# A convolution and mixture-of-experts chain on one core: the second expert product made token-major, with its outputs taken back through HBM

## The reference

```python
x = x + _L0_conv_ref(_gn(x), ...)      # 3x3 convolution, 8 to 8 channels, bias
x = x + _L1_conv_ref(_gn(x), ...)      # the same, other weights
h = jnp.einsum('bend,edf->benf', x, w1) + b1    # _L2: expert = channel, token = row
out = jnp.einsum('benf,efd->bend', gelu(h), w2) + b2   # d = 256 columns, f = 1024
x = x + _L3_conv_ref(_gn(x), ...)      # a third 3x3 convolution
```

## Time and profile before

| | us |
|---|---|
| median of 3 runs (lowest, highest) | 577.23 (575.82, 577.95) |
| the profiled execution's own time | 576.91 |
| its span, first to last instruction | 575.1 |
| PE / DVE / ACT / POOL busy | 520.0 / 374.1 / 291.8 / 159.1 |
| mean granted TensorE clock | 0.971 |

### The profile page before, as it was taken

The page is one execution under the profiler, slowest core; times in us unless marked ns, Lnnn a source line. Parts: engine busy times, 40 slices in busy tenths (PEclk is TensorE's granted clock), DMA queues, the critical chain, the costliest instruction groups (busy, mean ns, idle before and its releaser), DMA issues.

```text
span 575.1 us, 9042 instructions
## 1 busy us (share of the span) xinstructions
PE 520.0 (90%) x3326; PEld 255.5 (44%) x3326; DVE 374.1 (65%) x644; ACT 291.8 (51%) x354; POOL 159.1 (28%) x181
## 2 busy tenths in 40 slices
PE   0879999896979999999999999999999989978990
PEld 0534445364544444444444444444444545445440
DVE  4969999888766395194293392481547598678541
ACT  2599988333635453353362361461444828766510
POOL 4679888853270000000000000000000001677610
PEclk9889999898899999999999999999999999989996
DMA  8845555533020122022011112102123300134769
GB/s 327 324 111 146 150 132 139 143 101 147 0 75 1 73 74 74 0 73 73 0 73 73 31 42 73 73 0 73 74 74 108 112 0 2 45 81 107 242 200 349
DMA packets 14168, 57.41 MB, mean 100 GB/s; under 512 B 3116, under 2 KB 3244, under 8 KB 11052
## 3 DMA queue, kind: packets, MB, share of 16 engines
q1 hardware_dynamic: 11820, 49.30, 26.9%
q10 hardware_dynamic: 2316, 7.68, 3.7%
HBM read 30.03 MB, written 8.39 MB: 67 GB/s over the span
## 4 chain that ended last, share of the span: by engine, by line
PE 62%; DVE 19%; ACT 5%; POOL 4%; DMA 3%; issue 2%; ACTq 1%; SPq 1%; POOLq 0%; DVEq 0%
PE PS L1007 28%; PE PS L978 27%; DVE X L665 6%; DVE ST L626 6%; PE PS L878 2%; POOL XN L360 2%; ACT XN L439 2%; PE PS L952 2%; DMA X<-x 2%; PE PS L936 2%; PE PS L885 1%; DVE X L681 1%; ACT SCR L444 1%; DVE XT L674 1%; DVE SM L641 1%
## 5 line engine op out<-in xcount | busy, mean ns | idle before, releaser
L978 PE MATMUL PS<-XT,W1S 128*128 (+1 forms) x768 | 172.0, 383 | 1.7 <-DVE XT L674 1.7
L1007 PE MATMUL PS<-HID,W2S 128*128 128x512 f16 x768 | 170.8, 379 | 1.6 <-DVE W2S L688 1.6
L476 ACT ACTIVATE SCR<-PS,CONST 128x512 f32<-128x512 f32 x128 | 87.0, 686 | 64.4 <-PE PS L978 27.8
L978 PEld LDWEIGHTS PS<-XT,W1S 128*128 128x128 f16 x768 | 75.6, 99 | 91.1 <-issue 4.7
L1007 PEld LDWEIGHTS PS<-HID,W2S 128*128 128x128 f16 x768 | 75.1, 98 | 87.5 <-issue 1.8
L360 POOL TENSOR_TENSOR XN<-SCR,XN 128x1024 f16<-128x1024 f32 (+1 forms) x61 | 100.4, 1670 | 26.5 <-ACT SCR L444 26.5
L688 DVE SCALAR_TENSOR_TENSOR W2S<-W2F,W2S 128x2048 f16<-128x2048 f32 x10 | 22.9, 2291 | 114.6 <-ACT W2S L472 114.6
L333 POOL MEMSET HALO<- 48x520 f16 x12 | 6.3, 526 | 316.8 <-PE PS L978 316.3
L626 DVE BATCH_NORM_STATS2 ST<-X 128x6 f32<-128x512 f32 x128 | 81.5, 681 | 9.4 <-DMA X<-x 8.2
L439 ACT ACTIVATE XN<-X,SC 128x1024 f16<-128x1024 f32 (+1 forms) x61 | 64.1, 1050 | 33.9 <-POOL SC L351 27.6
L665 DVE SCALAR_TENSOR_TENSOR X<-PS,X 128x512 f32<-128x512 f32 x96 | 59.7, 680 | 21.5 <-PE PS L900 21.5
(11 more groups left out here) (47 smaller groups left out, 442.9 us busy)
## 6 DMA issues: line engine op xcount, KB each, us to landing
W1F<-w SPq DMA_DIRECT2D x10, 1024.0 KB, 4.7
W2F<-w SPq DMA_DIRECT2D x10, 1024.0 KB, 4.8
HALO<-XN SPq DMA_DIRECT2D x48, 129.9 KB
out<-X ACTq DMA_DIRECT2D x12, 512.0 KB, 6.8
HALO<-XN SPq DMA_DIRECT2D x48, 121.8 KB
X<-x SPq DMA_DIRECT2D x2, 2048.0 KB, 19.0
HALO<-XN SPq DMA_DIRECT2D x42, 64.9 KB
HALO<-XN SPq DMA_DIRECT2D x42, 60.9 KB
```

The source lines that it names most:

```text
L476: act.activation(SCR[:, ft % 2, 0:CH], bank(ft % G_RING), ACT.Gelu, bias=BT[:, ds(e * FT + ft, 1)], scale=1.0 / (XS * WS)).then_inc(gelu_o ...
L978: mm = pe.matmul(bank(ft % G_RING), W1S[:, w, h * NF + ft * P:h * NF + (ft + 1) * P], rhs, start=(n == 0), stop=(n == 3 * DH - 1))
L1007: mm = pe.matmul(bank(G2_BANK + h), W2S[:, w, ft * NW + h * P:ft * NW + (h + 1) * P], HID[slot][:, part, ft], start=(ft == 0 and part == 0 ...
```

## The change

**Second product.** `output` now takes HID's 128 tokens as the stationary operand and w2's 256 columns as the moving one: for each expert and pair four blocks (4 rows x 32 row groups of one image) of 24 matmuls with 256 columns, 1536 in all for 768 with 512. ScalarE copies each block out of PSUM (`copy_out`), 64 copies of 128x256 for 32 of 128x512. The bias is no longer in it: VectorE adds it to X, eight adds of a chunk for each image, in four of the loop's rounds (`add_bias`). XT's layout puts an expert's 256 tokens side by side; the writes into it, and the reads of PSUM for them, step differently.

**The way back.** SP stores each block to a new HBM tensor `yd` (64 DMAs of 128 KB, runs of 512 bytes). Whole rows come back: seven experts' rows of an image by two DMAs in ScalarE's queue, the last expert's by two in SP's, into a float32 image over the dead part of XT. `add_outputs` adds from there, all operands in SBUF. The result transposes are gone.

**The end.** The third convolution has seven PSUM banks in its ring for five. The first half's thirds of g = 8 to 11 are issued by ScalarE, all else of the halos by SP. All output stores are in SP's queue: image 0 and half of image 1 between the halos of g = 10 and 11, the rest after them.

```diff
-TT = 2 * NT
+NBLK = 2
+TOK = NBLK * P
+BLOCKS = 2 * NBLK
...
-L3_BANKS = (1, 2, 3, 0, 4)
+G2_BANK, TR_BANK, STAT_BANK, LAST_STAT_BANK = 4, 6, 5, 6
+L3_BANKS = (1, 2, 3, 0, 7, 4, 5)
...
-THIRDS_BY_ACT = ((0, 0), (11, 0), (11, 1),)
+THIRDS_BY_ACT = ((0, 0), (8, 0), (9, 0), (10, 0), (11, 0))
...
-    XT = at("XT", XY_OFF, [P, NPAIR, TT, DH, NC, 2, R], F16)
-    YT = at("YT", XY_OFF, [P, NPAIR, TT, DH, NC, R], F32)
+    XT = at("XT", XY_OFF, [P, NB, DH, NE, 2, TOK], F16)
+    YT = at("YT", XY_OFF, [P, NB, NBLK, NE, NW], F32)
+    YX = at("YX", XY_OFF, [P, NB * IMG], F32)
...
+        b, t = m // NCH, m % NCH * TC
+        return XT[:, b, :, :, part].rearrange("p w c (r t) -> p (w c) r t", r=R)[:, :, :, t:t + TC]
     def tr_bank(m):
-        return bank(TR_BANK + m % 2).rearrange("p (k r) -> p k r", r=R)
-
-    def yt_part(e, p, dh):
+        return bank(TR_BANK + m % 2).rearrange("p (t k r) -> p k r t", t=TC, r=R)
...
+    def y_image(b):
+        return YX[:, (0, 1, 0, 3)[b] * IMG:((0, 1, 0, 3)[b] + 1) * IMG]
...
+    def load_outputs(queue, b, rows):
+        queue.dma_start(y_image(b)[rows], yd[b][rows]).then_inc(y_in[b], 16)
+    def load_first_experts(queue, b):
+        for w in range(W2):
+            load_outputs(queue, b, slice(w * HALF_P, (w + 1) * HALF_P - R))
+    def load_last_expert(queue, b):
+        for w in range(W2):
+            load_outputs(queue, b, slice((w + 1) * HALF_P - R, (w + 1) * HALF_P))
...
+        def store_tokens(src, b, k, e, signal):
+            rows = yd[b].rearrange("(w c k r) (t j) -> c k (r t) w j", w=W2, c=NC, k=NBLK, j=NJ)
+            dst = rows[e, k]
+            sp.dma_start(dst, src.rearrange("p (w j) -> p w j", w=W2)).then_inc(signal, 16)
+        def store_outputs(e, p, first):
+            for k in range(BLOCKS):
+                sp.wait_ge(yt_ok, first + k + 1)
+                store_tokens(y_tokens(e, p, k), 2 * p + k // NBLK, k % NBLK, e, y_out[p])
+        def store(b, first):
+            for i in range(first, first + QUAD, 2):
+                sp.wait_ge(x_new, X_NEW_AT["c", 8 + b, i + 1])
+                sp.dma_start(out[b][:, i * CH:(i + 2) * CH], x_chunk(b, i, 2)
+                             ).then_inc(out_done, 16)
+        def store_last(n, k):
+            p = ENDING[n][1]
+            b = 2 * p + k // NBLK
+            sp.wait_ge(yt_ok, BLOCKS * (NPAIR * LAST + n) + k + 1)
+            store_tokens(y_last(p, k), b, k % NBLK, NE - 1, last_out[b])
...
-        for e in range(1, NE + 2):
+        for e in range(1, LAST + 1):
             load_w1(e)
             load_w2(e)
-        for g in range(8, 12):
-            if g < 8 + SLOTS:
-                load_ones(SLOT[g])
-            halos(g)
+            for p in range(NPAIR):
+                store_outputs(e - 1, p, BLOCKS * (NPAIR * (e - 1) + p))
+        load_w1(LAST + 1)
+        load_w2(LAST + 1)
+        store_outputs(LAST, 0, BLOCKS * NPAIR * LAST)
+        load_w1(LAST + 2)
+        load_w2(LAST + 2)
+        for k in range(BLOCKS):
+            store_last(1, k)
+        for b in range(2):
+            sp.wait_ge(last_out[b], 16 * NBLK)
+            load_last_expert(sp, b)
+        load_w1(LAST + 3)
+        load_w2(LAST + 3)
+        store_outputs(LAST, 1, BLOCKS * (NPAIR * LAST + 2))
+        load_ones(0)
+        store_last(3, 0)
+        store_last(3, 1)
+        sp.wait_ge(last_out[2], 16 * NBLK)
+        load_last_expert(sp, 2)
+        halo_half(8, 0)
+        store_last(3, 2)
+        store_last(3, 3)
+        halo_half(8, 1)
+        sp.wait_ge(last_out[3], 16 * NBLK)
+        load_last_expert(sp, 3)
+        load_ones(SLOT[9])
+        halos(9)
+        load_ones(SLOT[10])
+        halos(10)
+        store(0, 0)
+        store(0, QUAD)
+        store(1, 0)
+        halos(11)
+        store(1, QUAD)
+        store(2, 0)
+        store(2, QUAD)
...
+        def copy_out(to, k, done):
+            act.wait_ge(g2_mm, done)
+            act.activation(to, bank(G2_BANK + k % 2)[:, 0:NW], ACT.Copy,
+                           scale=1.0 / (HS * WS)).then_inc(yt_ok, 1)
...
+        def first_experts(b, p):
+            if b != 2:
+                act.wait_ge(g1_mm, 16 * LAST + FT * (2 * p + 2))
+            act.wait_ge(y_out[p], 16 * BLOCKS * (NE - 1))
+            load_first_experts(act, b)
...
+                if (k, ft) == (3, 3):
+                    act.wait_ge(x_new, X_NEW_AT["y", 0, NCH - 1])
+                    first_experts(2, 1)
+            if k == 1:
+                first_experts(0, 0)
+                first_experts(1, 0)
+            elif k == 3:
+                first_experts(3, 1)
...
         slot_free(8)
         normalise_piece(FIRST_PIECE[8])
+        ending_out(3, 0)
         normalise_piece(FIRST_PIECE[8] + 1)
-        ending_result(3, 0)
+        ending_out(3, 1)
         normalise_piece(FIRST_PIECE[8] + 2)
         normalise_piece(FIRST_PIECE[8] + 3)
-        ending_result(3, 1)
+        ending_out(3, 2)
+        thirds(8, 0)
         normalise_piece(FIRST_PIECE[8] + 4)
-
...
-        for g in range(9, 11):
-            normalise(g)
-        store(0)
-        slot_free(11)
-        for k in range(4):
-            normalise_piece(FIRST_PIECE[11] + k)
-        last_thirds(0)
-        normalise_piece(FIRST_PIECE[11] + 4)
-        last_thirds(1)
-        for b in range(1, NB - 1):
-            store(b)
+        ending_out(3, 3)
+        for g in range(9, 12):
+            slot_free(g)
+            for k in range(4):
+                normalise_piece(FIRST_PIECE[g] + k)
+            thirds(g, 0)
+            normalise_piece(FIRST_PIECE[g] + 4)
...
+        def add_outputs(b, i):
+            if i == 0:
+                dve.wait_ge(y_in[b], 16 * 2 * W2)
             xc = x_chunk(b, i)
-            dve.wait_ge(ty_mm, m + 1)
-            dve.tensor_tensor(xc, bank(TR_BANK + m % 2), xc, ALU.add).then_inc(x_new, 1)
+            dve.tensor_tensor(xc, y_chunk(b, i), xc, ALU.add).then_inc(x_new, 1)
+        def mlp_stats(b, i):
             dve.wait_ge(x_new, X_NEW_AT["y", b, i])
-            stats_chunk(12 + b, xc, i)
+            stats_chunk(12 + b, x_chunk(b, i), i)
+        def add_half(b, first):
+            for i in range(first, first + QUAD):
+                add_outputs(b, i)
+            for i in range(first, first + QUAD):
+                mlp_stats(b, i)
+        def add_bias(e):
+            for i in range(NCH):
+                xc = X[:, ds(e * IMG - (IMG - i * CH), CH)].rearrange("p (t j) -> p t j", j=NJ)
+                dve.tensor_tensor(xc, xc, B2.unsqueeze(1).broadcast_to([P, TC, NJ]), ALU.add
+                                  ).then_inc(bias_ok, 1)
...
+            tokens = slice(k * P, (k + 1) * P)
+            to = bank(G2_BANK + k % 2)
             for ft in range(FT):
...
-                for part, w in ((0, 0), (1, 0), (0, 1)):
-                    mm = pe.matmul(bank(G2_BANK + h),
-                                   W2S[:, w, ft * NW + h * P:ft * NW + (h + 1) * P],
-                                   HID[slot][:, part, ft],
-                                   start=(ft == 0 and part == 0 and w == 0),
+                for part, w in PRODUCTS:
+                    mm = pe.matmul(to[:, 0:NW], HID[slot][:, part, ft, tokens],
+                                   W2S[:, w, ft * NW:(ft + 1) * NW],
+                                   start=(ft == 0 and part == w),
                                    stop=(ft == FT - 1 and w == 1))
+                if ft == FT - 1:
+                    mm.then_inc(g2_mm, 1)
                 if between is not None:
-                    if ft == FT - 1:
-                        mm.then_inc(g2_mm, 1)
-                    between(ft)
...
+        for n, (e, p, _) in enumerate(ENDING):
+            hidden(e, p, in_fourth_hidden if n == 3 else None, n)
+            for k in range(BLOCKS):
+                output(e, p, k, in_fourth_output if n == 3 else None, n)
+        for g in range(8, 12):
             before_step(g)
             for i in range(0, NCH, QUAD):
-                last_centres(g, i, None)
+                for k in range(QUAD):
+                    if g < 10 and i + k == NCH - 1:
+                        group_mean(g + 6)
+                    centre(g, i + k)
+                    if (g, i, k) == (8, 0, 0):
+                        group_variance(13)
+                if g < 10 and i > 0:
+                    group_variance(g + 6)
                 tiles(g, i)
```

More of the change, by code:

```diff
@@ L1022, in expert @@
             for p in range(NPAIR):
-                for h in range(DH):
-                    output(e, p, h)
+                for k in range(BLOCKS):
+                    output(e, p, k)
         pe.wait_ge(cst_in, 16)
```

373 lines of the change are left out of this document (160 added, 213 removed).

## The result

Four runs of the changed kernel gave 606.12 us (605.93 to 606.66), four of the kernel before 576.85 us (575.82 to 577.95). The ratio is 1.051, with a 95% interval of 1.049 to 1.053: slower, as forecast, but by 29 us where 5.5 were worked out, and outside the range of 572 to 591.

The account below looks back on a forecast made before the run. TensorE was taken to bound the loop, a ScalarE-GpSimd ring the third convolution and stores the end. Span 580.6 + 1.8 = 582.4 against 576.91, +5.5; 582.7 in the median's terms, range 572 to 591.

Parts of the forecast that it names:

- Step 1: Second product's stream: 1536 matmuls of 256 columns at 110 ns with weight loads hidden, +2.4 us up to the ending.
- Step 2: Loop's copies (0.5 us each), bias adds and 64 stores all hidden; XT's writes taken to cost nothing more.
- Step 3: Four ending parts up to the last hidden product: 77.5 us with stalls, ending at 485.9, a gain of 0.9 us.
- Step 4: Third convolution's ScalarE-GpSimd ring: four halo issues add 2.7 us per image for three images; last low part ends at 558.9.
- rival (a): Third convolution's ring is not lengthened, the halo issues being hidden: 8 us less there, time 573.3, faster; chance 0.20.
- Step 5: Last halo and stores: halos land 3 us later, updates end at 571.6, stores run until 576.9, span 580.6.
- (b): Third convolution's ring: half of the lengthening hidden, 578.0 us, no change; chance 0.17.
- Rival (c): Weight loads show in the output stream (598 at 120 ns) or XT's writes double (593); together 0.07.
- Rival (d): VectorE's SBUF adds and GpSimd's low parts lock each other out, 5.4 us into the ring: 588; chance 0.06.
- Rival (e): Image 2's last rows return late, some 6 us trip; each us beyond 503 costs one; within forecast's range, no separate chance.

Follow-up runs that it names:

- e1: Changed kernel without the round trip: no stores or loads of rows, VectorE adds the chunk to itself; 585.38 us.
- e8: e1 with the third convolution's halo issues and output stores back in the queues used before the change; 580.29 us.
- e4: Changed kernel with the third convolution's halo issues and output stores back in the queues used before the change; 599.53 us.
- e11: VectorE alternates adds and statistics for images 2 and 3, against a combined kernel with image 2's load split (583.00 us); 580.60 us.
- e15: e14 with image 3's last stores ahead of the first image's halo issues and its load between their halves; 579.60 us, ratio 1.0049.
- e12: e11 with ScalarE taking the last ending part's first two output copies before the first normalisation piece, the other two earlier; 580.35 us, ratio 1.0074.
- e13: e12 with image 2's bulk load asked for earlier, over before the last expert's stores; 579.58 us, ratio 1.0047.
- e6: Changed kernel without 56-partition bulk loads: each image returns in one 128-partition load after its last stores land; 592.84 us.
- e14: e12 with image 2 loaded whole behind its stores and no bulk load; 579.57 us.
- e9: Adds as scalar_tensor_tensor instead of tensor_tensor, against a kernel combining the orders of e2, e3, e4 and e6's whole loads (585.97 us); 582.39 us.
- e2: Changed kernel with the last ending part's weight loads ahead of SyncE's waits for the landed stores; 602.71 us.
- e3: Changed kernel with image 1's variance ahead of the first adds of image 2 on VectorE; 602.74 us.
- e5: Changed kernel with VectorE's first adds of image 0 after the third ending part's splits and the next weight split; 608.31 us.

## Why the prediction was wrong

The direction, the loop and the ring were right; the trip was not.

- *Step 1, the output stream.* 109.2 ns a matmul for the 110 taken, 20.96 us a stage. Weight loads (99 ns) stayed hidden. The formula of the Trainium skill, "TensorE: Matmul & The Clock Gate", section "Back-to-back issue gap", gives 109.2 for 256 columns, though the section means it for a single matmul alone. The rows of this stream agree with it.
- *Step 2.* XT's writes still took 684 ns, the 256-wide copies 384 ns, where I had taken 500, and the bias adds had no idle time before them. Its clause on the stores, that SP has nothing else waiting but weight loads, needed a stage later, is true of the loop only.
- *Step 3, the four parts.* Without the trip the stalls were sized well: e1 begins the last output at 484.4, where the forecast, less 1.9 us for the loads' issues that e1 does not make, has 484.0. That its first piece then came at 489.1, near the 490.1 forecast, is in part luck. It waited 2.97 us for GpSimd's scale, which the forecast did not have (2.01 before), and e1 does not make the issues for which the forecast had 3.1 us. With the trip the piece came at 501.9. I had gone through part 3 for what is late next and found the splits, but not that the change puts two new waits there: VectorE's for the rows, ahead of the last splits, and SyncE's for the landed stores, ahead of the weights. With what followed from these two the first piece came 11.8 us later than forecast, and 14.6 later than in e1 if both are counted from the split (314.4 and 299.8).
- *Step 4, the ring.* The four issues between the fourth and fifth piece cost what was forecast (2.7 to 2.8 us). e1's distances sum to 56.1 us for the 53.5 forecast, and its last low part ends 17.8 us after the last first piece instead of 15.3, as the halo issues there took 5.31 us for 2.7. SyncE issues six output stores just before (from 549.1 us) and its own halo copies beside them, and the stores I had not counted: with the end as before (e8) it is 15.3 us again (541.18 to 556.50). That these stores are the reason is likely and not shown, as e8 moves the issues too. Undone, the two moves together give back 6.4 us (e8) or 7.6 (e4), where the three images of rival (a) had 8.
- *Step 5.* From the end of the last low part to the end of the span: 20.5 us in e1 and 20.5 in the changed kernel, for 21.7. It was 1.2 us too long. Rivals (a) and (b) are refuted with step 4.
- *Rival (c)* is refuted by the rows of steps 1 and 2. *Rival (d)*, adds and low parts locked, is real and had too small a chance: VectorE's adds of images 2 and 3 do fall beside low parts. In e8 it is where the loss against the kernel before lies, and e11 took 3.2 us of it away by order alone. In the last versions it is the likeliest reason of what is left (e15's rows); no run is free of it. The row that it rested on, is a step of a group's scale on 128x1, not a subtraction.
- *Rival (e), the step that failed.* It had one of the two right places and a wrong size. I took "some 6 us" for store, landing and load; in the changed kernel it was 9.22 + 0.33 + 6.55 us, from a copy that came late itself, and the rows of image 2 arrived at 523.3. For images 0 and 1 the sum had nothing, and there the trip cost the 11.8 us of step 3. In all it is worth 22.1 us (e1). The rate, "each us beyond 503 is a us", is not borne out in the one pair that bears on it (its end as before): between e12 and e13 the rows came 7.7 us sooner, 2.0 of them beyond 503, and the stretch is 0.2 shorter. I counted the bytes of the DMA in the loop and never asked what the bulk loads do to the small stores sharing the DMA engines with them. Rival (e) deserved a chance and a price of its own.
- *In sum.* The span is 603.8 us for the 580.6 forecast, 23.2 too long: 19.0 by the trip (22.1 for the 3.1 forecast), 5.8 by the other steps (e1 against the forecast, both from the split), less 1.6 as the split came earlier (187.5 for 189.1).

The cause of that size is shown by e6, e12, e13 and e14. A load of 56 partitions moved 193 to 195 GB/s with a busy share of 0.87 to 0.88; loads of 128 partitions (rows and weights) 410 to 429 at 0.97 to 1.01. While such a load lasts, a small store in another queue is late: 8.0 us for 1.9. How the engines share their time between the two queues, no run shows. The Trainium skill, "SBUF — State Buffer", section "Door 1: The DMA port swizzle", says that partitions 0 to 63 reach only 8 of the 16 ports that DMA has into SBUF, and gives 196 GB/s for such a transfer of 1 MiB; its part on issuing two transfers for the two halves says that they do not add up. Both agree with the rows. The Trainium skill, "DMA: Bandwidth & Descriptors", section "Why a DMA increments its semaphore by 16 and not by 1", has a transfer run on the largest number of engines up to 16 that divides its partitions; for 56 that is 14 of 16, a share of 0.875 (an estimate by that rule). The rows have that share. The prediction weighed neither, and the first speaks against loads of 56 partitions.

The Trainium skill, "SBUF — State Buffer", section "Who interferes with whom", has the lock between VectorE and GpSimd. By that rule e9 had to be without effect, since the form of the operation is not in it, and it was.

## What to carry over

A round trip through memory is priced by what shares the DMA engines with it when it matters, not by its bytes. An early partial load at half of the rate can be worth less than one late load at the full rate. For each wait that a change adds, list what stands behind it on that queue: here hidden splits on VectorE and weight loads on SyncE.

When several waits lie behind one slow resource, taking away one of them shows 0.8 to 4.2 us (e2, e3, e5) and can look like a refutation. Take the resource's load away (e6) before the waits.

## What was not expected of the hardware

- A 128 KB store landed after 8.0 us beside 56-partition loads in the other queue, and after 1.9 without them; in the changed kernel it was up to 17.4 us. Behind a load of 128 partitions in its own queue it was 4.8 and 7.7 us.
- Beside the low parts, four adds that take 2.48 us alone took 7.17 (e3) and 8.09 (e8), 4.7 and 5.6 us more, between two and three low parts of 2.07 us. In the changed kernel a GpSimd scale step at 544.79 took 2.27 us for 0.56.
- A mark ahead of which all the kernels after the change do the same work lies within a band of 3.6 us, 187.1 to 190.7. A single run's difference below that says little until the stretch is taken from a common mark.
